# Scattered expert outputs and plainly loaded operands in a two-layer gated transformer kernel

## The reference, cut to what matters

```
x = x + tanh(g0) * cross_attention(layernorm(x), ctx)            # block-sparse, 16 heads
h = layernorm(x)
h = h + self_attention_0(ln1(h))                                 # causal, 16 heads
h = h + token_moe(ln2(h))      # each token: its 2 best of 8 experts, weights from a softmax
h = h + self_attention_1(ln1(h))
h = h + seq_moe(ln2(h))        # each sequence: its 2 best of 8 experts
x = x + tanh(g1) * h
x = x + tanh(g2) * mlstm(layernorm(x), ctx, ctx)
x = x + tanh(g3) * int8_linear(layernorm(x))
```

## Time and profile before

| what | value |
|---|---|
| three runs | 1061.59, 1054.81, 1050.97 us (median 1054.81) |
| the profiled execution | 1058.88 us, with a span of 1056.9 us |
| PE busy | 875.1 us, 83% of the span |
| DVE busy | 709.9 us, 67% |
| ACT busy | 689.9 us, 65% |
| POOL busy | 514.5 us, 49% |
| indirect gathers L789 | 71, 76.7 us on POOL |
| indirect fetches L799 | 64, 63.1 us on POOL |

### The profile page before, as it was taken

One profiled execution on the slowest core, in us unless ns is written; L12 is line 12 of the kernel. 1 busy time (PEld: TensorE's weight loads), 2 busy tenths in 40 slices (PEclk: granted clock), 3 DMA queues, 4 the chain that ended last, 5 costly groups with the idle time before them and its releaser, 6 DMA issues.

```text
span 1056.9 us, 34800 instructions
## 1 busy us (share of the span) xinstructions
PE 875.1 (83%) x11693; PEld 711.3 (67%) x11693; DVE 709.9 (67%) x1912; ACT 689.9 (65%) x1914; POOL 514.5 (49%) x893
## 2 busy tenths in 40 slices
PE   3999999999986599999458888975999998879804
PEld 2778878788875299999446776863777777747501
DVE  3488888888868856666458888768312122957795
ACT  2588888899973577777347887853555554448635
POOL 6133334566672155555389898411333332038616
PEclk9999999999997699999759999987999999979955
DMA  5000032000002022222211001800000001511002
GB/s 146 11 17 15 15 101 74 3 2 0 0 2 81 5 66 65 65 67 63 47 33 33 25 25 25 239 2 0 1 0 0 0 0 37 123 48 38 17 0 80
DMA packets 53195, 41.54 MB, mean 39 GB/s; under 512 B 11176, under 2 KB 45716, under 8 KB 53124
## 3 DMA queue, kind: packets, MB, share of 16 engines
q1 hardware_dynamic: 48220, 31.50, 10.8%
q0 software_dynamic: 4320, 8.86, 3.5%
q10 hardware_dynamic: 584, 0.26, 0.1%
HBM read 27.42 MB, written 9.24 MB: 35 GB/s over the span
## 4 chain that ended last, share of the span: by engine, by line
PE 56%; DVE 18%; POOLq 8%; issue 7%; POOL 6%; ACT 2%; SPq 2%; DMA 1%; DVEq 0%; ACTq 0%
PE ps_st L1207 14%; PE ps_o L1207 14%; PE ps_v L1309 8%; PE ps_xa L1207 8%; POOLq L830 5%; PE ps_v L1207 5%; PE ps_o L1331 3%; DVE work L1711 3%; POOL work L831 2%; POOLq L820 2%; DVE y L1725 1%; DVE recip L1722 1%; DVE stats L1650 1%; SPq L543 1%; POOL h_all L799 1%
## 5 line engine op out<-in xcount | busy, mean ns | idle before, releaser
L747 POOL TENSOR_TENSOR shared<-kts,kmask 128x256 f32<-128x256 f32 x192 | 135.9, 729 | 162.4 <-ACT qts L934 99.6
L1207 PE MATMUL ps_st<-work 128*128 128x128 f32 (+1 forms) x872 | 153.0, 319 | 16.7 <-POOL work L831 9.6
L1207 PEld LDWEIGHTS ps_st<-work 128*128 128x128 f32 x872 | 123.6, 191 | 40.5 <-POOL work L831 26.1
L965 ACT COPY probs_t<-ps_v 128x512 f32<-128x512 f32 x192 | 112.6, 586 | 47.8 <-PE ps_v L1309 45.8
L1703 DVE TENSOR_REDUCE rowmax<-ps_st 128x16 f32<-128x1024 f32 x96 | 117.2, 1221 | 28.3 <-PE ps_st L1207 26.0
L1309 PE MATMUL ps_v<-ident,work 128*128 128x128 f32 x768 | 123.5, 284 | 3.0 <-ACT probs_t L965 2.2
L1711 DVE TENSOR_TENSOR work<-ps_st,rowmax 128x1024 f32<-128x1024 f32 x96 | 116.5, 1214 | 0.1
L789 POOL DMA_INDIRECT xg<-x_rows,row_from x71 | 76.7, 1081 | 78.9 <-PE ps_xa L1393 59.0
L957 ACT ACTIVATE work<-work 128x512 f32<-128x512 f32 x192 | 110.4, 622 | 2.3
L1207 PE MATMUL ps_o<-shared,probs_t 128*64 128x18 f32 x3072 | 109.3, 212 | 0.5
L1102 ACT ACTIVATE probs_t<-ps_st,b1s 128x256 f32<-128x256 f32 x152 | 59.7, 476 | 73.2 <-PE ps_st L1207 73.2
(11 more groups left out here) (379 smaller groups left out, 2086.9 us busy)
## 6 DMA issues: line engine op xcount, KB each, us to landing
y_rows<-work SPq DMA_DIRECT2D x71, 64.0 KB, 1.6
w<-in_L_ffn_e_w_dram SPq DMA_DIRECT2D x2, 2048.0 KB, 11.4
w<-rhs_const SPq DMA_DIRECT2D x2, 1536.0 KB, 11.2
x_res<-in_x_dram SPq DMA_DIRECT2D x4, 512.0 KB, 6.6
ctx_in<-in_ctx_dram SPq DMA_DIRECT2D x32, 64.0 KB, 1.8
x_rows<-h_all SPq DMA_DIRECT2D x1, 2048.0 KB, 9.9
ctx_dup<-in_ctx_dram SPq DMA_DIRECT2D x32, 64.0 KB, 1.8
out_dram<-x_res SPq DMA_DIRECT2D x16, 128.0 KB, 1.8
```

The lines of the kernel that those rows point to most:

```text
L747: i = pool.tensor_tensor(km[:, par, g, :, :], kts[:, par, g:g + 1, :].to_broadcast([P, KM_HEADS, SEQ]), kmask[:, :, :], ALU.mult)
L965: nc.scalar.copy(probs_t[:, par, 512 * half:512 * half + 512], ps_v[:, :]).then_inc(S["pts_ready"], 1)
L1207: return nc.tensor.matmul(o, a, b, start=start, stop=stop, skip_group_check=True)
```

## The change

1. **Turns write to the tokens' places.** `y_d` now has two rows for each token (row 2n for its first choice, 2n + 1 for its second), and spare rows for the empty slots. `x_d` gets one spare row in its middle. From a second accumulation of one-hot products over the last four pieces (into `ps_o`) DVE works out `row_to` in three more small instructions. After the gather of turn t, POOL scatters the result of turn t - 6 by `row_to`. SP's 71 stores and POOL's copy `slot_of` are gone.
2. **Plain loads.** When all scatters have landed, SP issues 14 plain loads, in parts of 1, 1, 2, 4, 8, 8 and 8 tiles, each with one load for `y_first` and one for `y_second`. POOL has no fetches any more.
3. **Lags and order.** GROUP is 2, so LEAD is 5 and AHEAD 7. DVE's order is now: combine first, y, maximum, combine second, statistics of the combined tile, statistics of the updated tile, add, shift.
4. **The opening.** SP loads a quarter of x, two context tiles, the rest of x, and then context tiles 2 to 7 with five small loads behind each. DVE takes the statistics of 8 tiles before the first normalise, and those of the other 24 in rounds 1 to 4 of the attention, their means and roots in rounds 5 to 7. The setup pieces move from tiles 2 to 5 to tiles 8 to 11.
5. The store of the normalised rows to `x_d` is three transfers instead of one.

```diff
-YROWS = NTURN * TURN
+SPARE_ROW = TOK // 2
+FIRST_SPARE = 2 * (TOK + 1)
+YROWS = FIRST_SPARE + NTURN * TURN
...
-GROUP = 4
+GROUP = 2
...
-RING = 8
+Y_PARTS = (0, 1, 2, 4, 8, 16, 24, 32)
+SCATTER = 6
...
-        am_kept, am_spread = y_stored[1], y_stored[2:4]
+        am_kept, am_spread, AM0 = fetched[1], fetched[2:4], 32
...
-            pipeline(sp, [(0, ctx_load(0))])
+            first_ctx = ctx_load(0)
+            x_load(0)
+            first_ctx(0, 0)
+            first_ctx(1, 1)
+            for q in range(1, 4):
+                x_load(q)
+            for t in range(2, 2 * SUB):
+                first_ctx(t, t % 2)
+                late_loads(t - 2)
...
-            def turn_store(t, par, slot_):
-
-                sp.wait_ge(S["turn_y"], t + 1)
-                sp.dma_start(y_d[bass.ds(t * TURN, TURN), :], ty[:, slot_, :]).then_inc(y_stored[slot_], 16)
-            pipeline(sp, [(0, turn_store, XBUFS)], NTURN)
...
+            def outputs_load(part):
+
+                a, b = Y_PARTS[part], Y_PARTS[part + 1]
+                first_row = a * P + (1 if a * P >= SPARE_ROW else 0)
+                both = y_d.rearrange("(r k) d -> r k d", k=2)[first_row:first_row + (b - a) * P, :, :]
+                for k, dst in enumerate((y_first, y_second)):
+                    sp.dma_start(dst[:, a * D:b * D].rearrange("p (t d) -> p t d", d=D),
+                                 both[:, k, :].rearrange("(t p) d -> p t d", p=P)).then_inc(fetched[part], 16)
+
+            for b in range(XBUFS):
+                sp.wait_ge(y_stored[b], STORED[b])
+            for part in range(len(Y_PARTS) - 1):
+                outputs_load(part)
...
-            def fetch(t, par):
-
-                if t == 0:
-                    pool.wait_ge(S["slots_cast"], 1)
-                seen(pool, S["second_done"], t - RING + 1)
-                for c, dst in enumerate((y_first, y_second)):
-                    pool.indirect_dma_start(tile(dst, t), None, y_d, bass.IndirectOffsetOnAxis(slot_of[:, c, t:t + 1], 0)
-                                            ).then_inc(fetched[t % RING], 16)
+            def scatter(t):
+
+                pool.wait_ge(S["turn_y"], t + 1)
+                pool.indirect_dma_start(y_d, bass.IndirectOffsetOnAxis(row_to[:, t:t + 1], 0), ty[:, t % XBUFS, :], None
+                                        ).then_inc(y_stored[t % XBUFS], 16)
...
-            for t in range(NTURN):
-                gather(t)
-            pool.wait_ge(S["turn_out"], NTURN)
-            for b in range(XBUFS):
-                pool.wait_ge(y_stored[b], 16 * len(range(b, NTURN, XBUFS)))
-            straight([(LEAD, normalise), (AHEAD, kbd_after_scores), (AHEAD - 1, four_biases), (0, fetch)])
+            for t in range(NTURN + SCATTER):
+                if t < NTURN:
+                    gather(t)
+                if t == SCATTER:
+                    pool.wait_ge(S["rows_known"], 4)
+                if t >= SCATTER:
+                    scatter(t - SCATTER)
+            straight([(LEAD, normalise), (AHEAD, kbd_after_scores), (AHEAD - 1, four_biases)])
...
+                if k >= PIECES // 2:
+                    for j in range(COLS):
+                        i = mm(ps_o[:, 0:NTURN], onehot_b[:, k % 4, j, :], onehot_a[:, k % 2, j, :],
+                               k == PIECES // 2 and j == 0, k == PIECES - 1 and j == COLS - 1)
...
-                dve.wait_ge(fetched[t % RING], 32 * (t // RING + 1))
+                dve.wait_ge(fetched[next(k for k in range(len(Y_PARTS)) if t < Y_PARTS[k + 1])], 32)
...
-            row_stats(CH_CROSS, NT)
+            row_rstd(CH_CROSS, 0, FIRST)
...
-                    {3: small_weights,
+                    {1: lambda: x_sums(FIRST, FIRST + 6), 2: lambda: x_sums(FIRST + 6, FIRST + 12),
+                     3: lambda: x_sums(FIRST + 12, FIRST + 18), 4: lambda: x_sums(FIRST + 18, NT),
+                     5: lambda: row_means(CH_CROSS2, NT, FIRST, NT), 7: lambda: row_rstd(CH_CROSS2, FIRST, NT),
+                     9: small_weights,
...
-            straight(later([sums_, y_, max_, add_, shift_], LEAD)
-                     + [(LAND, combine_first), (LAND, combine_second), (LAND, fetched_stats)])
+            straight([(LAND, combine_first)] + later([y_, max_], LEAD) + [(LAND, combine_second), (LAND, fetched_stats)]
+                     + later([sums_, add_, shift_], LEAD))
```

More of the change, by code:

```diff
@@ L185, in chained @@
     for seg in range(len(segments)):
-        stop = seg * n + head + (SEAM if seg else 0)
+        stop = seg * n + head + (SEAM if seg else opening)
         while i < stop:
@@ L366, in build @@
         turn_of = sb("turn_of", [1, NTURN], I32)
-        slot_of = sb("slot_of", [P, 2, NT], U32)
+        second_side = sb("second_side", [P, NTURN])
+        spare_no = sb("spare_no", [P, NTURN])
+        row_to = sb("row_to", [P, NTURN], U32)
         row_from = sb("row_from", [P, NTURN], U32)
@@ L410, in build @@
         ps_v = psum("ps_v", 512)
-        x_d = nc.dram_tensor("x_rows", (TOK, D), F32, kind="Internal").ap()
+        x_d = nc.dram_tensor("x_rows", (TOK + 1, D), F32, kind="Internal").ap()
         y_d = nc.dram_tensor("y_rows", (YROWS, D), F32, kind="Internal").ap()
@@ L531, in build @@
         N_WLOADS = len(small_loads)
+        LATE_EACH = -(-N_WLOADS // (2 * SUB - 2))
         @block.sync
@@ L587, in _ @@
+            with sp.Fori(SUB, NT // 2, 1) as turn:
+                for u in range(2):
+                    first_ctx(turn * 2 + u, u)
             expert_load(0)
             sp.wait_ge(S["xn_ready"], PRE0 + NT)
-            sp.dma_start(x_d.rearrange("(t p) d -> p t d", p=P), h_t.rearrange("p (t d) -> p t d", d=D)
-                         ).then_inc(S["xa_stored"], 16)
-            def turn_store(t, par, slot_):
-                sp.wait_ge(S["turn_y"], t + 1)
-                sp.dma_start(y_d[bass.ds(t * TURN, TURN), :], ty[:, slot_, :]).then_inc(y_stored[slot_], 16)
@@ L597, in _ @@
-            pipeline(sp, [(0, turn_store, XBUFS)], NTURN)
+            for half in range(2):
+                first_row = half * (SPARE_ROW + 1)
+                sp.dma_start(x_d[first_row:first_row + TOK // 2, :].rearrange("(t p) d -> p t d", p=P),
+                             h_t[:, half * (TOK // 2):(half + 1) * (TOK // 2)].rearrange("p (t d) -> p t d", d=D)
+                             ).then_inc(S["xa_stored"], 16)
+            sp.dma_start(x_d[SPARE_ROW:SPARE_ROW + 1, :], h_t[0:1, 0:D]).then_inc(S["xa_stored"], 16)
@@ L694, in routing_constants @@
                                 allow_small_or_imprecise_dtypes=True))
-                fresh(pool.iota(row_no[:, :], pattern=[[P, NT]], base=-HALF_ROW, channel_multiplier=1,
+                for half in range(2):
+                    fresh(pool.iota(row_no[:, half * (NT // 2):(half + 1) * (NT // 2)], pattern=[[P, NT // 2]],
+                                    base=half - (1 - half) * SPARE_ROW, channel_multiplier=1,
+                                    allow_small_or_imprecise_dtypes=True))
+                fresh(pool.iota(spare_no[:, :], pattern=[[TURN, NTURN]], base=FIRST_SPARE - 2 * SPARE_ROW, channel_multiplier=1,
                                 allow_small_or_imprecise_dtypes=True))
@@ L1939, in combine_second, with x_sums @@
                                        ALU.mult, ALU.add).then_inc(S["second_done"], 1)
-            for q in range(4):
-                dve.wait_ge(x_loaded[q], 16)
-                for t in range(q * (NT // 4), (q + 1) * (NT // 4)):
-                    sums_step(x_res)(t, 0)
+            def x_sums(a, b):
+                for q in range(4):
+                    part = range(max(a, q * (NT // 4)), min(b, (q + 1) * (NT // 4)))
+                    if part:
+                        dve.wait_ge(x_loaded[q], 16)
+                    for t in part:
+                        sums_step(x_res)(t, 0)
+            x_sums(0, FIRST)
+            row_means(CH_CROSS, FIRST, 0, FIRST)
             dve.wait_ge(S["setup_copied"], 3)
             V.tensor_scalar(coef[:, 0:1], tg[:, 0:1], ROW0_PAIRS, None, ALU.mult).then_inc(S["dve_setup"], 1)
-            row_stats(CH_CROSS, NT)
+            row_rstd(CH_CROSS, 0, FIRST)
             dve.wait_ge(S["dve_setup"], 1)
```

62 lines of the change are left out of this document (33 added, 29 removed).

## The result

The changed kernel takes 1070.41 us (median of 4 runs, 1069.11 to 1073.2) beside 1056.95 us of the kernel before (4 runs, 1050.97 to 1061.59): ratio 1.0127, 95% interval 1.0074 to 1.018. Forecast was 1067 us. Measured once more at the end it was 1068.69 against 1057.30, ratio 1.0098 (1.0069 to 1.0127). It is slower by about 1%, the likeliest case of the forecast.

What follows compares the result with a forecast made beforehand. PE was taken to bound the turns, POOL and DVE the second self-attention. Terms +43 - 14 - 2 - 10 - 5 = +12 us on 1058.9 gave 1071, or 1067 us against the median; own range 1050 to 1084, 1035 to 1098 at 0.8.

Steps and rivals of the forecast that it cites:

- Part 1: In the expert turns, scatters added to POOL's gathers make a turn 2.70 us instead of 1.994: +43 us.
- the instructions for `row_to`: Before the turns, DVE's three added instructions are needed only six gathers later and cost nothing.
- Part 2: Between the last scatter's landing and shift 0 of the second self-attention, 15.6 us instead of 30.0: -14 us.
- the -2: Second self-attention, shift 0 to shift 3: 14.7 us instead of 16.7, with POOL no longer in the way.
- Part 3: In the second self-attention, a tile takes 4.5 us instead of 5.00 once fetches are gone: -10 us.
- the loop "scores, maximum, combining, the statistics and the add, shift": In the second self-attention, this chain through the single `ps_st` sets the pace: 4.4 us, 4.5 with signals.
- POOL and DVE were both near 5.0 us: Second self-attention before the change, per tile: POOL by its work, DVE by its work and a 0.6 us out-projection wait.
- Part 4: In the opening, the 3.25 us context-tile wait goes and setup pieces run at full clock: -5 us (0 to -9).
- (a): In the turns, a cheap scatter fits POOL's 0.9 us slack; at 0.5 us the time is 1035; chance 0.20.
- (b): In the turns, the scatter costs 1.4 us or its landing holds `ty`: +75 us, 1099 us; chance 0.08.
- (c): In the turns, PE at 73% busy loses full clock for a third of the stage: 1102 us; chance 0.10.
- (d): In the turns, each POOL transfer waits for one whole DVE copy: 3.32 us a turn, 1118 us; chance 0.05.

Runs made afterwards that it cites:

- plain loads: The changed kernel with the turns' inputs loaded by SP, 128 rows in a row, instead of gathered by index on POOL, scatters kept: 1033.4 us.
- third order: The changed kernel with DVE's self-attention steps as y, both combines with statistics, then maximum, add, shift: 1093.42 us, ratio 1.0214.
- cut copies: The changed kernel with DVE's two expert-weight copies cut to one column each from the fifth turn on, run twice: 1102.7 and 1100.2 us.
- doubled scatters: The changed kernel with each turn's scatter issued twice, the second to a tensor nobody reads, run twice: 1203.4 and 1203.08 us.
- without POOL's bias: The kernel before with new opening, groups of 2, y-first DVE order and fetches, second self-attention's output bias moved to PE: 1059.15 us, ratio 0.9902.

## Why the prediction was right

**Part 1, the turns.** Right in mechanism and size. Forecast were 142 transfers of 1.35 us and a landing 193 us behind the first gather, measured 191.2: +41.5 against +43. The rows of the gathers priced the scatter, 1.00 us on average against 1.05, and the 0.30 us behind it. What made it cheaper than 2.70 us a turn is that the first scatter follows six gathers and the last six have none beside them; in between, scatters are 2.66 us apart. The plain loads show that hardly anything but the shared queue makes the cost. One small item was wrong: the instructions for `row_to` were put at nothing. In all eight traces with them and the gathers the first gather starts 0.9 us behind `row_from`, right behind the last of them, and in all five without them 0.30 us: 0.6 us, though the code makes only the scatters wait for them. Why the gather waits isn't known. And from the first gather to the first bias add it is 9.2 us, not 4.3; with six turns between it costs nothing (the scatters wait 1.8 us for results in all).

**Part 2, the wait.** -14 forecast, -14.1 measured. For shifts 0 to 3 14.7 us were forecast, and 13.6 measured in one profile and 16.8 in the other: the -2 isn't shown, and that the first came near it was the clock. The run with groups of 2 and fetches shows that 5.0 us of it could be had without the scatter.

**Part 3, the pace.** The sign was right, the term was mis-sized: 4.73 us a tile instead of 4.5, -5.1 instead of -10. The failed step is the loop "scores, maximum, combining, the statistics and the add, shift". It left out that PE's weighing waits for the add, through `ps_o`, and that the scores stand behind the weighing. But that alone makes no difference, since the weighing ends only 0.04 us behind the shift. The loop through the shift is itself 4.69 us long, because its terms were taken too short: scores 0.95 us instead of 0.8, the other tile's statistics and the add 0.46 instead of 0.3, the signals 0.2 instead of 0.1, and the second combine 0.12 longer beside POOL's product, though the combining as a whole (0.73) stayed under the 0.9 allowed for it. That POOL and DVE were both near 5.0 us was read rightly; the old order without fetches shows DVE's side to be enough by itself. How much POOL's side alone would have held the kernel before stays open.

**Part 4, the opening.** -5 forecast; 7.3 at the first gather in the one trace, 4.9 by the medians of the opening alone and 3.1 by its ratio. The forecast can't be told from any of them.

**The sum.** Forecast was +12 us; it is +10.5 between the two traces, +13.5 between the medians and +11.4 in the repetition. That is nearer than the terms are: in the traces part 3 was 5 us too hopeful, and parts 1, 2 and 4 together as much too careful, partly by the clock's rise in one execution. That these cancel is luck; the size of part 1, which decides the sign, isn't.

**The rivals.** (a) needed a scatter under 0.78 us; none of 71 is under 0.97. (b) and its landing: the bias adds wait 0.8 us in all for it. (c) The clock stayed at 1.00 with PE at 81%. With late signals and 2.97 to 2.99 us a turn PE was busy 72 to 74% of 370 to 560 us, the share that this rival had named, and the clock was 0.94 to 0.95; at 60% it was 0.79. So the rival's fall exists, but the changed kernel didn't reach it. (d) The period would have been 3.32 us, it is 2.58. What this rival had wrong is where the transfers start, not the lock: a transfer waits for the rest of the copy in which it starts, 0.2 us or so for most gathers and nothing for 66 of 71 scatters. A rule of the Trainium skill (SBUF — State Buffer, "SBUF: two separate sides") has GpSimd unable to write descriptors while DVE runs such a copy. The traces agree with it: 48 gathers of the kernel before end within 0.01 us of the same distance behind the copy's end.

A version that beats both kernels is the opening with groups of 2, stores by SP and fetches by index as before: 1048.92 us, 0.9915. It keeps what the scatter isn't needed for.

## What to carry to other kernels

A transfer by index costs its issuing engine the whole duration and a gap behind it (here 1.0 + 0.30 us), whoever waits for the data; before moving one, add up the queue that it moves into, in the stage where it will stand. Moving 64 fetches out of a wait and putting 71 scatters into a stage with 0.9 us of slack a turn gave back 14 us and cost 41. And when two engines both look full at the same pace, undo the relief of one alone: with the old order of DVE's steps taking the fetches off POOL gave nothing, with the third order it did. In a loop over engines, every buffer's last reader has to be followed, not only the buffer that seems scarce. And where an instruction of DVE takes two lengths in one trace, look at what POOL does when it starts.

## What the runs showed of the hardware

- In five runs (both with cut copies, both with doubled scatters, the third order), PE's results were taken by ACT, DVE and POOL about 2 us late in every second or third turn, and by up to 10 us with three transfers a turn. In the two other runs made beside a kernel before of 1070 us the same shows without a second transfer in the turns: once in the turns without POOL's bias (the transposed tile of 366.1 us, 1.5 us late), and in six tiles of the second self-attention with it. In the seven traces where the kernel before took 1057 to 1059 us (its own, the changed kernel twice, the old order, the plain loads, the opening with groups of 4 and of 2) it never does. Cause open.
- A second combine on DVE (two operands in SBUF) that starts while POOL's mask product runs ends 0.15 us behind that product: after 0.47 us in the changed kernel, 0.62 with the third order and fetches, 0.88 in every second tile of the third order without them. Started 0.07 to 0.12 us ahead of the product it takes 0.33 to 0.34 us, and alone 0.35. No run moved the product by itself, but the distance is the same in three kernels.
- A transfer by index that starts within a weight copy of DVE ends 0.82 to 0.88 us behind that copy's end, gather or scatter; outside, the median is 0.97 us for a gather and 0.99 for a scatter.
- PE's clock held 1.00 at 81% busy with gaps of about half a microsecond in each turn, was 0.94 to 0.95 on average at 72 to 74% with gaps of up to 3.6 us, and 0.79 at 60%.
